# Attention stage of a fused kernel: probability tiles turned three slots behind their scores and ahead of the products, the scalar engine copying head 2 of four

## The chip, the cores and the metric

The kernel runs on one core of a Trainium2 chip. The metric is the device time of one launch in microseconds. Five engines work side by side and meet only at semaphores: TensorE (PE; its weight loads are listed as PEld), VectorE (DVE), ScalarE (ACT), GpSimd (POOL) and the DMA queues, most of which SyncE (SP) issues here.

## The reference

One launch computes a cross-attention, a mixture of 64 experts, a second attention over the context and a dense feed-forward layer, on 8 batches of 256 tokens of width 512. The change lies in the first attention alone, 16 heads of width 32:

```python
q = rms_norm(linear(x, q_w, q_b), norm_q_w).reshape(B, L, NH, HD)
k_img = rms_norm(linear(ctx_img, k_img_w, k_img_b), norm_k_img_w).reshape(B, -1, NH, HD)
v_img = linear(ctx_img, v_img_w, v_img_b).reshape(B, -1, NH, HD)
scores = jnp.einsum('bqhd,bkhd->bhqk', q, k) * scale
probs = jax.nn.softmax(scores, axis=-1)
return jnp.einsum('bhqk,bkhd->bqhd', probs, v)
```

The context has 256 rows, all of them inside the first 257, so only the image branch has keys; the text branch is empty and adds nothing.

## The kernel before

The program is a row of stages (project, attend, route, place, experts, finish), each a block that all engines leave before the next begins. The change is inside `attend`, which in the profile lasts from 220.6 to 422.1 us.

`attend` works on 32 units (8 batches times 4 groups of four heads). A unit is done in two slots of two heads each, so there are 64 slots. For one slot `s` these steps follow each other:

- PE `scores` (line 319): four fp32 matmuls with 32 rows of contraction, two query halves of two heads, into `pS[s % 2]`; they wait until ACT has read slot `s - 2`.
- DVE `tensor_reduce` (361): the minimum of the negated scores, step "M".
- ACT (395): four exponentials with their sums into `prob[s % 4]`, step "E".
- DVE `reciprocal` (366), step "R", written one slot later in DVE's program.
- POOL (415): two multiplications of `prob` by the reciprocal, one for each head, steps "N0" and "N1".
- PE `turn` (330): two halves (head 0 and head 1 of the slot) of four 128x128 transposes each, into `pT[0]` and `pT[1]`. Each half waits for POOL's step and until the half before it in the same `pT` has been copied out.
- the copies from `pT` to `probT`: DVE (375) or ACT (388).
- PE `products` (340), once for each unit, when all four heads lie in `probT`: eight fp32 matmuls with 32 output columns each into `pO`.
- ACT (404): `pO` to `qT`, whose columns are free by then.

Each engine's program is written out by hand as a loop over slots; nothing reorders it. What stands behind a waiting instruction on its engine waits too. Before the change PE does, in slot `s`: `scores(s)`, then in odd slots `products` of unit `(s - 1) / 2 - 2`, then `turn(s - 2)`. DVE does M of `s`, R of `s - 1`, then the copies of slot `s - 2`; of the four heads of a unit it copies heads 0, 1 and 2. ACT copies head 3, which lies in `pT[1]`, at the head of the even slots (three slots behind), then does its exponentials.

In slots 8 to 11 ACT also does a copy of one quarter of the output weights (line 400), and in slots 12 to 15 POOL does the subtraction that goes with it (419). SP meanwhile writes 64 blocks of zeros and moves the weights of the last layer to another place in memory; these transfers wait for nothing in the loop over slots.

`Steps` counts a semaphore for one engine's named steps; `wait(eng, unit, name)` waits until the step of that unit has been done.

Of the kernel before, what the change touches and what calls it, by code (L numbers as in the profile page):

```python
# [28 lines left out]
ACT = mybir.ActivationFunctionType  # L29
# [4 lines left out]
T = B * S  # L34
# [4 lines left out]
HG = P // HD  # L39
# [209 lines left out]
def attend(nc, a, qT, kT, V, Wraw, Wo, ident, y_dram, ffn_gu, ffn_d):  # L249
# [3 lines left out]

    GH, PAIR, UNITS = range(HG), 2, B * DC
    PAIRS = HG // PAIR
    SLOTS, BUFS = UNITS * PAIRS, 4
    slots = range(SLOTS + 5)
    with ExitStack() as ctx:
        sb = lambda name, shape, dt=F32: ctx.enter_context(nc.sbuf_tensor(name, shape, dt))
# [3 lines left out]
        probT = sb("probT", [P, 2, HG, TPB, S])  # L263
        pS = [ps(f"pS{i}", [P, PAIR, TPB, S]) for i in range(2)]
        pT = [ps(f"pT{j}", [P, TPB, S]) for j in range(PAIR)]
        pO = [ps(f"pO{j}", [P, S]) for j in range(2)]
        peS, peO = Steps(nc, ctx, "a_peS", ["S"]), Steps(nc, ctx, "a_peO", ["O"])
        peT = Steps(nc, ctx, "a_peT", ["T0", "T1"])
        dveM, dveR = Steps(nc, ctx, "a_dveM", ["M"]), Steps(nc, ctx, "a_dveR", ["R"])
        dveT, actT = Steps(nc, ctx, "a_dveT", ["T0", "T1", "T2"]), Steps(nc, ctx, "a_actT", ["T3"])  # L270
        actE, actO = Steps(nc, ctx, "a_actE", ["E"]), Steps(nc, ctx, "a_actO", ["O"])
        poolN = Steps(nc, ctx, "a_poolN", ["N0", "N1"])
        zero, s_zero, s_rest = sb("zero", [P, D]), ctx.enter_context(nc.semaphore("a_zero")), ctx.enter_context(nc.semaphore("a_rest"))
# [6 lines left out]
        @block.sync  # L280
        def _(eng):


            eng.dma_start(Wraw[:, :, :], a["attn_wT"][3]).then_inc(s_wo, 16)
            rest = y_dram.rearrange("(n p) d -> n p d", p=P)[T * K // P:NBLK]
            eng.wait_ge(s_zero, 1)
            for n in range(NBLK - T * K // P):
                eng.dma_start(rest[n], zero[:, :]).then_inc(s_rest, 16)

            half = DC * F  # L290
            eng.dma_start(ffn_gu[:, 0:half], a["ffn_gT"].rearrange("p c f -> p (c f)")).then_inc(s_words, 16)
            eng.dma_start(ffn_gu[:, half:2 * half], a["ffn_uT"].rearrange("p c f -> p (c f)")).then_inc(s_words, 16)
            eng.dma_start(ffn_d, a["ffn_dT"].rearrange("p f d -> p (f d)")).then_inc(s_words, 16)
            eng.wait_ge(s_rest, 16 * (NBLK - T * K // P))
            eng.wait_ge(s_words, 48)

        def place_of(s):
            u, x = divmod(s, PAIRS)
            return u, x, u // DC, u % DC

        def turned(eng, u, j):

            if j < HG - 1:
                dveT.wait(eng, u, f"T{j}")
            else:
                actT.wait(eng, u, "T3")

        @block.tensor
        def _(eng):
            for x in (peS, peT, peO):  # L310
                x.start(eng)

            def scores(s):
                u, x, b, g = place_of(s)
                actE.wait(eng, s - 2, "E")
                for h in range(TPB):
                    for i in range(PAIR):
                        rows = bass.ts(x * PAIR + i, HD)
                        m = eng.matmul(pS[s % 2][:, i, h, :], qT[rows, g, b * S + h * P:b * S + (h + 1) * P], kT[rows, g, bass.ts(b, S)],
                                       start=True, stop=True)  # L320
                peS.done(m, "S")

            def turn(s):
                u, x, b, g = place_of(s)
                for i in range(PAIR):
                    poolN.wait(eng, s, f"N{i}")
                    turned(eng, (s - 1) // PAIRS, (s - 1) % PAIRS * PAIR + i)
                    for kt in range(TPB):
                        for h in range(TPB):
                            m = eng.transpose(pT[i][:, kt, bass.ts(h, P)], prob[:, s % BUFS, i, h, bass.ts(kt, P)], ident[:, :])  # L330
                    peT.done(m, f"T{i}")

            def products(u):
                b, g = u // DC, u % DC
                actO.wait(eng, u - 2, "O")
                for j in GH:
                    turned(eng, u, j)
                for kt in range(TPB):
                    for j in GH:
                        m = eng.matmul(pO[u % 2][bass.ts(j, HD), :], V[:, b * TPB + kt, g * P + j * HD:g * P + (j + 1) * HD],  # L340
                                       probT[:, u % 2, j, kt, :], start=kt == 0, stop=kt == TPB - 1)
                peO.done(m, "O")

            for s in slots:
                if s < SLOTS:
                    scores(s)
                if s % PAIRS == 1 and 0 <= s // PAIRS - 2 < UNITS:
                    products(s // PAIRS - 2)
                if 0 <= s - 2 < SLOTS:
                    turn(s - 2)  # L350

        @block.vector
        def _(eng):
            for x in (dveM, dveR, dveT):
                x.start(eng)

            for s in slots:
                if s < SLOTS:
                    peS.wait(eng, s, "S")
                    actE.wait(eng, s - BUFS, "E")  # L360
                    dveM.done(eng.tensor_reduce(low[:, s % BUFS, :, :], pS[s % 2][:, :, :, :], axis=AX.X, op=ALU.min), "M")  # L361
                r = s - 1
                if 0 <= r < SLOTS:
                    actE.wait(eng, r, "E")
                    poolN.wait(eng, r - BUFS, "N1")
                    dveR.done(eng.reciprocal(inv[:, r % BUFS, :, :], tot[:, r % BUFS, :, :]), "R")  # L366
                c = s - 2
                if 0 <= c < SLOTS:
                    u, x, b, g = place_of(c)
                    for i in range(PAIR):  # L370
                        j = x * PAIR + i
                        if j < HG - 1:
                            peT.wait(eng, c, f"T{i}")
                            peO.wait(eng, u - 2, "O")
                            dveT.done(eng.tensor_copy(probT[:, u % 2, j, :, :], pT[i][:, :, :]), f"T{j}")

        @block.scalar
        def _(eng):
            for x in (actE, actT, actO):
                x.start(eng)  # L380

            for s in slots:
                c = s - 3
                if 0 <= c < SLOTS and c % PAIRS == PAIRS - 1:
                    u, x, b, g = place_of(c)
                    peT.wait(eng, c, f"T{PAIR - 1}")
                    peO.wait(eng, u - 2, "O")
                    actT.done(eng.activation(probT[:, u % 2, HG - 1, :, :], pT[PAIR - 1][:, :, :], ACT.Copy), "T3")
                if s < SLOTS:
                    dveM.wait(eng, s, "M")  # L390
                    peT.wait(eng, s - BUFS, f"T{PAIR - 1}")
                    dveR.wait(eng, s - BUFS, "R")
                    for i in range(PAIR):
                        for h in range(TPB):
                            e = eng.activation(prob[:, s % BUFS, i, h, :], pS[s % 2][:, i, h, :], ACT.Exp, bias=low[:, s % BUFS, i, h:h + 1],  # L395
                                               scale=-1.0, accum_out=tot[:, s % BUFS, i, h:h + 1])
                    actE.done(e, "E")
                if s in HIGHS:
                    eng.wait_ge(s_wo, 16)
                    eng.activation(Wo[0][:, s - HIGHS[0], :], Wraw[:, s - HIGHS[0], :], ACT.Copy).then_inc(s_high, 1)  # L400
                if s % PAIRS == 0 and 0 <= s // PAIRS - 3 < UNITS:
                    u = s // PAIRS - 3
                    peO.wait(eng, u, "O")
                    actO.done(eng.activation(qT[:, u % DC, bass.ts(u // DC, S)], pO[u % 2][:, :], ACT.Copy), "O")
# [1353 lines left out]
```

## Time and profile before

| | us |
|---|---|
| median of three runs | 1659.73 |
| the runs | 1667.11, 1659.73, 1653.78 |
| the profiled execution | 1676.87 |
| its span | 1675.0 |
| `attend` within it | 201.5 |
| PE busy over the span | 1470.4 |
| DVE, ACT, POOL busy over the span | 1026.8, 869.5, 630.1 |

How to read it: the durations in the rows below are those of the profiled execution, which is 17.1 us longer than the median of the runs. The three runs lie 13.3 us apart. A busy PE is not PE at its peak, since the ends of pipelined matmuls are modelled; the distance from one start to the next is what the engine's program took. "Idle before" names the releaser that came last by the profile. The chain that ended last, part 4 of the page, covers 30% of the span and lies in the last stage, so it says nothing of `attend`. TensorE's granted clock is 1.00 at full speed, which is 2.4 GHz, and 0.50 at 1.2 GHz.

### The profile page before, as it was taken

The page shows a single profiled execution, that of the slowest core. Times are in us where ns is not written, and L with a number is a line of the kernel's source. Part 1 is how long each engine was busy: PE and PEld are TensorE (multiplying, and loading weights), DVE is VectorE, ACT ScalarE, POOL GpSimd, SP SyncE. Part 2 cuts the span into 40 slices and gives each one's busy share as a digit, 9 for nine tenths or more (in the row PEclk, how much of TensorE's full clock was granted, in tenths as well). Part 3 has the DMA queues.
Part 4 walks back from the last instruction along what each step waited for, and adds up shares of the span by engine and source line. Part 5 has one row for each costly group of instructions (what it writes and reads, how often), then busy time and mean ns, then how long its engine had stood idle before and what let it go on. Part 6 is the DMA issues. An engine that isn't in the chain of part 4 may idle for free. (4 is left out here: it accounts for less than half of the span.)

```text
span 1675.0 us, 37963 instructions
## 1 busy us (share of the span) xinstructions
PE 1470.4 (88%) x8537; PEld 1170.0 (70%) x8538; DVE 1026.8 (61%) x2055; ACT 869.5 (52%) x1988; POOL 630.1 (38%) x717
## 2 busy tenths in 40 slices
PE   2999989999884399999999999999981579999999
PEld 1545555665672298888888888888871468888888
DVE  3343446787568757667677666666634456667732
ACT  0222247888337556666666666666640234444442
POOL 2212136777114232232223323222316476666322
PEclk9999968999995599999999999999995789999999
DMA  5000079000117158877877777777637444444200
GB/s 225 25 19 25 19 275 359 2 1 2 48 57 295 44 166 280 276 270 261 277 268 266 270 263 248 263 252 263 221 109 251 130 148 134 138 135 135 81 13 26
DMA packets 90247, 273.83 MB, mean 163 GB/s; under 512 B 12421, under 2 KB 12550, under 8 KB 88966
## 3 DMA queue, kind: packets, MB, share of 16 engines
q1 hardware_dynamic: 66070, 191.80, 32.5%
q0 software_dynamic: 23680, 77.61, 15.4%
q10 hardware_dynamic: 432, 3.67, 0.5%
q8 instruction: 26, 0.43, 0.1%
q14 instruction: 39, 0.32, 0.1%
HBM read 204.88 MB, written 76.81 MB: 168 GB/s over the span
## 5 line engine op out<-in xcount | busy, mean ns | idle before, releaser
L974 POOL DMA_INDIRECT xg<-h_rows,idx x168 | 184.8, 1100 | 463.6 <-PE m_x L1002 454.4
L1017 PE MATMUL m_g<-wgu_high,bxTh 128*128 x660 | 236.2, 358 | 2.2 <-DVE bxTl L1090 2.1
L1017 PE MATMUL m_g<-wgu_low,bxTh 128*128 x660 | 223.5, 339 | 0.0
L1017 PE MATMUL m_g<-wgu_high,bxTl 128*128 x660 | 223.3, 338 | 0.0
L1420 PE MATMUL f_g<-x4T_high,ffn_gu 128*128 128x256 f32 x704 | 176.5, 292 | 14.5 <-issue 12.2
L1420 PE MATMUL f_g<-x4T_low,ffn_gu 128*128 128x256 f32 x704 | 169.3, 282 | 0.0
L1090 DVE TENSOR_TENSOR bxTl<-m_x,bxTh 128x512 fp32r<-128x512 f32 x166 | 114.8, 692 | 84.6 <-ACT bxTh L1159 64.2
L852 DVE TENSOR_TENSOR wgu_low<-raw_gu,wgu_high x61 | 107.3, 1759 | 82.9 <-ACT wgu_high L842 81.7
L1311 POOL DMA_INDIRECT G<-y_rows,slot x128 | 135.3, 1057 | 56.6 <-issue 50.5
L415 POOL TENSOR_TENSOR prob<-prob,inv 128x512 f32<-128x512 f32 x128 | 130.5, 1041 | 62.8 <-DVE inv L366 62.8
L1177 ACT ACTIVATE y<-m_y 128x512 f32<-128x512 f32 x164 | 98.3, 600 | 105.9 <-PE m_y L1037 91.1
L1037 PE MATMUL m_y<-wd_high,hidTm 128*128 x328 | 144.4, 440 | 7.6 <-issue 5.2
L1420 PEld LDWEIGHTS f_g<-x4T_high,ffn_gu 128*128 128x128 f32 x704 | 134.5, 191 | 20.4 <-issue 16.8
L395 ACT ACTIVATE prob<-pS,low 128x256 f32<-128x256 f32 x256 | 118.1, 475 | 44.8 <-DVE low L361 44.8
L1420 PEld LDWEIGHTS f_g<-x4T_low,ffn_gu 128*128 128x128 f32 x704 | 134.7, 191 | 2.0 <-issue 1.7
L1037 PE MATMUL m_y<-wd_low,hidTm 128*128 x328 | 129.9, 396 | 0.0
L1017 PEld LDWEIGHTS m_g<-wgu_high,bxTh 128*128 128x128 f32 x660 | 124.4, 188 | 3.4 <-issue 2.8
L1017 PEld LDWEIGHTS m_g<-wgu_low,bxTh 128*128 128x128 f32 x660 | 124.9, 189 | 0.0
L1017 PEld LDWEIGHTS m_g<-wgu_high,bxTl 128*128 128x128 f32 x660 | 124.5, 189 | 0.0
L1159 ACT ACTIVATE bxTh<-m_x 128x512 fp32r<-128x512 f32 x166 | 99.1, 597 | 47.6 <-issue 45.2
L1474 DVE SCALAR_TENSOR_TENSOR X<-G,w,X 128x512 f32 (+1 forms) x128 | 106.1, 869 | 15.3 <-DMA G<-y_rows,slot 14.6
L1317 POOL TENSOR_TENSOR hT_low<-f_hid,hT_high 128x256 fp32r<-128x256 f32 x88 | 66.7, 759 | 116.8 <-ACT hT_high L1658 115.7
(240 smaller groups left out, 3222.4 us busy)
## 6 DMA issues: line engine op xcount, KB each, us to landing
raw_gu<-in_exp_gu SPq DMA_DIRECT2D x64, 768.0 KB, 6.8
y_rows<-y SPq DMA_DIRECT2D x164, 256.0 KB
raw_d<-in_exp_d SPq DMA_DIRECT2D x64, 512.0 KB, 7.7
y_rows<-zero SPq DMA_DIRECT2D x64, 256.0 KB, 3.5
ffn_gu<-ffn_gu_words SPq DMA_DIRECT2D x1, 5632.0 KB
X<-in_x SPq DMA_DIRECT2D x4, 1024.0 KB, 17.8
ctxT<-in_ctxT SPq DMA_DIRECT2D x16, 256.0 KB, 2.6
h_rows<-h SPq DMA_DIRECT2D x16, 256.0 KB, 2.0
```

What stands on the lines that cost most here:

```text
L395: e = eng.activation(prob[:, s % BUFS, i, h, :], pS[s % 2][:, i, h, :], ACT.Exp, bias=low[:, s % BUFS, i, h:h + 1], scale=-1.0, accum_out= ...
L415: poolN.done(eng.tensor_tensor(w, w, inv[:, s % BUFS, i, :].unsqueeze(2).to_broadcast([P, TPB, S]), ALU.mult), f"N{i}")
L852: eng.tensor_tensor(self.gu[1][:, at, :], self.raw_gu[:, at, :], self.gu[0][:, at, :].bitcast(F32), ALU.subtract).then_inc(self.s_low_gu, 1)
L974: eng.indirect_dma_start(xg[:, u, :].bitcast(F32), None, h_dram, bass.IndirectOffsetOnAxis(ap=idx[half][:, u:u + 1], axis=0)).then_inc(s_g ...
L1017: m = eng.matmul(pg[u % 2][:, 0:2 * I], xT[l][:, u % 2, c, :], W.gu[r][:, buf * DC + c, :], start=c == 0 and n == 0, stop=c == DC - 1 and ...
L1037: m = eng.matmul(py[par][:, :], left, right, start=n == 0, stop=n == 4)
L1090: dveX.done(eng.tensor_tensor(xT[1][:, u % 2, :, :], px[u % 2][:, :].rearrange("p (c n) -> p c n", c=DC), xT[0][:, u % 2, :, :].bitcast(F3 ...
L1159: actX.done(eng.activation(xT[0][:, u % 2, :, :], px[u % 2][:, :].rearrange("p (c n) -> p c n", c=DC), ACT.Copy), "xTh")
L1177: actY.done(eng.activation(y[:, u % 2, :], py[u % 2][:, :], ACT.Copy), "y")
L1311: eng.indirect_dma_start(G[:, i, k, :], None, y_dram, bass.IndirectOffsetOnAxis(ap=slot8[:, t, k:k + 1], axis=0)).then_inc(s_g[i][k], 16)
L1420: m = eng.matmul(pgu[f % 2][:, bass.ts(n, S)], Wgu[:, n, c, bass.ts(f, P)].bitcast(way), x[:, c, :].bitcast(way), start=c == 0 and part == ...
L1474: dveA.done(eng.scalar_tensor_tensor(X[:, t, :], G[:, i, k, :], w8[:, t, k:k + 1], X[:, t, :], ALU.mult, ALU.add), f"k{k}_{i}")
```

## The change

PE turns slot `s - 3` in slot `s`, and does so right after the scores; the products come last in the odd slots. DVE's copies go along and are three slots behind too. ACT copies head 2 of each unit (in `pT[0]`) and DVE heads 0, 1 and 3. ACT's copy was three slots behind the scores already: it stood one slot behind its turn and now stands in the same slot as its turn.

```diff
--- before.py
+++ after.py
@@ -253,7 +253,9 @@
 
     GH, PAIR, UNITS = range(HG), 2, B * DC
     PAIRS = HG // PAIR
-    SLOTS, BUFS = UNITS * PAIRS, 4
+    SLOTS, BUFS, TURN = UNITS * PAIRS, 4, 3
+
+    ACT_HEAD = 2
     slots = range(SLOTS + 5)
     with ExitStack() as ctx:
         sb = lambda name, shape, dt=F32: ctx.enter_context(nc.sbuf_tensor(name, shape, dt))
@@ -267,7 +269,7 @@
         peS, peO = Steps(nc, ctx, "a_peS", ["S"]), Steps(nc, ctx, "a_peO", ["O"])
         peT = Steps(nc, ctx, "a_peT", ["T0", "T1"])
         dveM, dveR = Steps(nc, ctx, "a_dveM", ["M"]), Steps(nc, ctx, "a_dveR", ["R"])
-        dveT, actT = Steps(nc, ctx, "a_dveT", ["T0", "T1", "T2"]), Steps(nc, ctx, "a_actT", ["T3"])
+        dveT, actT = Steps(nc, ctx, "a_dveT", [f"T{j}" for j in GH if j != ACT_HEAD]), Steps(nc, ctx, "a_actT", [f"T{ACT_HEAD}"])
         actE, actO = Steps(nc, ctx, "a_actE", ["E"]), Steps(nc, ctx, "a_actO", ["O"])
         poolN = Steps(nc, ctx, "a_poolN", ["N0", "N1"])
         zero, s_zero, s_rest = sb("zero", [P, D]), ctx.enter_context(nc.semaphore("a_zero")), ctx.enter_context(nc.semaphore("a_rest"))
@@ -300,10 +302,7 @@
 
         def turned(eng, u, j):
 
-            if j < HG - 1:
-                dveT.wait(eng, u, f"T{j}")
-            else:
-                actT.wait(eng, u, "T3")
+            (actT if j == ACT_HEAD else dveT).wait(eng, u, f"T{j}")
 
         @block.tensor
         def _(eng):
@@ -344,10 +343,10 @@
             for s in slots:
                 if s < SLOTS:
                     scores(s)
+                if 0 <= s - TURN < SLOTS:
+                    turn(s - TURN)
                 if s % PAIRS == 1 and 0 <= s // PAIRS - 2 < UNITS:
                     products(s // PAIRS - 2)
-                if 0 <= s - 2 < SLOTS:
-                    turn(s - 2)
 
         @block.vector
         def _(eng):
@@ -364,12 +363,12 @@
                     actE.wait(eng, r, "E")
                     poolN.wait(eng, r - BUFS, "N1")
                     dveR.done(eng.reciprocal(inv[:, r % BUFS, :, :], tot[:, r % BUFS, :, :]), "R")
-                c = s - 2
+                c = s - TURN
                 if 0 <= c < SLOTS:
                     u, x, b, g = place_of(c)
                     for i in range(PAIR):
                         j = x * PAIR + i
-                        if j < HG - 1:
+                        if j != ACT_HEAD:
                             peT.wait(eng, c, f"T{i}")
                             peO.wait(eng, u - 2, "O")
                             dveT.done(eng.tensor_copy(probT[:, u % 2, j, :, :], pT[i][:, :, :]), f"T{j}")
@@ -380,12 +379,12 @@
                 x.start(eng)
 
             for s in slots:
-                c = s - 3
-                if 0 <= c < SLOTS and c % PAIRS == PAIRS - 1:
+                c = s - TURN
+                if 0 <= c < SLOTS and c % PAIRS == ACT_HEAD // PAIR:
                     u, x, b, g = place_of(c)
-                    peT.wait(eng, c, f"T{PAIR - 1}")
+                    peT.wait(eng, c, f"T{ACT_HEAD % PAIR}")
                     peO.wait(eng, u - 2, "O")
-                    actT.done(eng.activation(probT[:, u % 2, HG - 1, :, :], pT[PAIR - 1][:, :, :], ACT.Copy), "T3")
+                    actT.done(eng.activation(probT[:, u % 2, ACT_HEAD, :, :], pT[ACT_HEAD % PAIR][:, :, :], ACT.Copy), f"T{ACT_HEAD}")
                 if s < SLOTS:
                     dveM.wait(eng, s, "M")
                     peT.wait(eng, s - BUFS, f"T{PAIR - 1}")
```

The order on PE, in the middle of the stage. `pS` are the scores, `pT` the turned probabilities, `pO` the products; `a_actT` and `a_dveT` are the copies out of `pT` by ACT and DVE, `a_poolN` the multiplications, `a_actE` the exponentials. Before, from the products of an odd slot to the turn of the even slot behind it:

```order
L340 MATMUL pO0<-probT,V 32x256 [waits a_dveT,a_actT,a_actO]
L340 MATMUL pO0<-probT,V 32x256 x7
L330 MATMUL pT0<-ident,prob 128x128 [waits a_dveT,a_poolN]
L330 MATMUL pT0<-ident,prob 128x128 x3
L330 MATMUL pT1<-ident,prob 128x128 [waits a_dveT,a_poolN]
L330 MATMUL pT1<-ident,prob 128x128 x3
L319 MATMUL pS0<-kT,qT 128x256 [waits a_actE]
L319 MATMUL pS0<-kT,qT 128x256 x3
L330 MATMUL pT0<-ident,prob 128x128 [waits a_dveT,a_poolN]
L330 MATMUL pT0<-ident,prob 128x128 x3
L330 MATMUL pT1<-ident,prob 128x128 [waits a_actT,a_poolN]
L330 MATMUL pT1<-ident,prob 128x128 x3
```

And with the change, from the turn of an odd slot to the turn of the even slot behind it:

```order
L329 MATMUL pT0<-ident,prob 128x128 [waits a_actT,a_poolN]
L329 MATMUL pT0<-ident,prob 128x128 x3
L329 MATMUL pT1<-ident,prob 128x128 [waits a_dveT,a_poolN]
L329 MATMUL pT1<-ident,prob 128x128 x3
L339 MATMUL pO0<-probT,V 32x256 [waits a_actT,a_dveT,a_actO]
L339 MATMUL pO0<-probT,V 32x256 x7
L318 MATMUL pS0<-kT,qT 128x256 [waits a_actE]
L318 MATMUL pS0<-kT,qT 128x256 x3
L329 MATMUL pT0<-ident,prob 128x128 [waits a_dveT,a_poolN]
L329 MATMUL pT0<-ident,prob 128x128 x3
L329 MATMUL pT1<-ident,prob 128x128 [waits a_dveT,a_poolN]
L329 MATMUL pT1<-ident,prob 128x128 x3
```

The products have moved from ahead of the odd slot's turn to behind it. The wait on ACT's copy has moved from the second half (`pT1`) of the even slot's turn to the first half (`pT0`) of the odd slot's turn.

The order on ACT, from an odd slot's exponentials over one even slot. Before:

```order
L395 ACTIVATE prob,tot<-pS1,low 128x256 [waits a_dveR,a_peT,a_dveM]
L395 ACTIVATE prob,tot<-pS1,low 128x256 x3
L388 ACTIVATE probT<-pT1 128x512 [waits a_peO,a_peT]
L395 ACTIVATE prob,tot<-pS0,low 128x256 [waits a_dveR,a_peT,a_dveM]
L395 ACTIVATE prob,tot<-pS0,low 128x256 x3
L404 ACTIVATE qT<-pO1 128x256 [waits a_peO]
```

And with the change:

```order
L394 ACTIVATE prob,tot<-pS1,low 128x256 [waits a_dveR,a_peT,a_dveM]
L394 ACTIVATE prob,tot<-pS1,low 128x256 x3
L387 ACTIVATE probT<-pT0 128x512 [waits a_peO,a_peT]
L394 ACTIVATE prob,tot<-pS0,low 128x256 [waits a_dveR,a_peT,a_dveM]
L394 ACTIVATE prob,tot<-pS0,low 128x256 x3
L403 ACTIVATE qT<-pO1 128x256 [waits a_peO]
```

The rows stand in the same order; the copy reads `pT0` in place of `pT1`, and its wait on the turning is for the slot that PE works on at the same time.

## Rows read from the trace of the kernel before

**Rows 1.** Windows: stretch, length, busy PE, PEld, DVE, ACT, POOL; PEclk, DMA share, GB/s.

```profile
220.60:422.10 201.50, 188.53 (x1536) 121.62 (x1536) 143.89 (x224) 151.70 (x581) 135.44 (x133) 0.90 0.38 133
224.00:261.00 37.00, 35.95 (x174) 23.23 (x175) 17.84 (x29) 20.60 (x82) 17.68 (x18) 0.50 1.04 393
261.00:291.76 30.76, 27.89 (x237) 17.63 (x236) 22.02 (x34) 23.11 (x87) 23.80 (x23) 0.94 1.03 347
291.76:414.21 122.45, 118.04 (x1060) 76.51 (x1056) 98.55 (x155) 101.80 (x396) 89.66 (x88) 1.00 0.02 6
```

**Rows 2.** Waits, 292 to 414 us: us in total, times, longest us.

```profile
PEld pT L330 <- POOL prob L415: 9.0, 22, 0.4
...
PE pT L330 <- ACT probT L388: 4.4, 22, 0.2
```

**Rows 3.** Timeline, PE, one unit: start us, us, engine, line, operation [idle before].

```profile
337.31 1.13 PE L319 MATMUL pS<-kT,qT 32*128 32x256 f32 x8
338.37 0.66 PE L330 MATMUL pT<-ident,prob 128*128 128x128 f32 x4
339.23 0.63 PE L330 MATMUL pT<-ident,prob 128*128 128x128 f32 x4 [0.20 <-ACT probT L388]
339.79 1.13 PE L319 MATMUL pS<-kT,qT 32*128 32x256 f32 x8
340.85 1.07 PE L340 MATMUL pO<-probT,V 128*32 128x256 f32 x16
341.85 1.09 PE L330 MATMUL pT<-ident,prob 128*128 128x128 f32 x8
342.88 0.48 PE L319 MATMUL pS<-kT,qT 32*128 32x256 f32 x2
```

**Rows 4.** Timeline of the weight loads (PEld), same stretch.

```profile
341.85 0.86 PEld L330 LDWEIGHTS pT<-ident,prob 128*128 128x128 f32 x8 [0.41 <-issue]
342.88 0.30 PEld L319 LDWEIGHTS pS<-kT,qT 32*128 32x128 f32 x4 [0.17 <-issue]
```

**Rows 5.** Timeline, DVE, same stretch.

```profile
338.49 1.23 DVE L361 TENSOR_REDUCE low<-pS 128x4 f32<-128x1024 f32 x1 [0.82 <-PE pS L319]
339.63 0.17 DVE L366 RECIPROCAL inv<-tot 128x4 f32<-128x4 f32 x1
339.71 1.26 DVE L375 COPY probT<-pT 128x512 f32<-128x512 f32 x2
...
342.55 0.69 DVE L375 COPY probT<-pT 128x512 f32<-128x512 f32 x1 [0.27 <-PE pT L330]
```

**Rows 6.** Timeline, ACT, same stretch.

```profile
338.48 0.61 ACT L388 ACTIVATE probT<-pT 128x512 f32<-128x512 f32 x1
339.75 0.47 ACT L395 ACTIVATE prob<-pS,low 128x256 f32<-128x256 f32 x1 [0.66 <-DVE low L361]
```

**Rows 7.** Timeline, POOL, 336 to 343 us.

```profile
336.79 2.04 POOL L415 TENSOR_TENSOR prob<-prob,inv 128x512 f32<-128x512 f32 x2 [0.44 <-DVE inv L366]
339.88 2.04 POOL L415 TENSOR_TENSOR prob<-prob,inv 128x512 f32<-128x512 f32 x2 [1.05 <-DVE inv L366]
```

**Rows 8.** Line 419: count, ns min/median/max, first and last start.

```profile
L419 POOL TENSOR_TENSOR wo_low<-wo_raw,wo_high x4: 1262/1266/1271, 274.7 to 285.8; 128x512 fp32r<-128x512 f32 x4
```

**Rows 9.** Timeline, PE, head of the stage.

```profile
225.04 2.08 PE L319 MATMUL pS<-kT,qT 32*128 32x256 f32 x8 [3.25 <-ACT prob L395]
...
236.77 2.08 PE L319 MATMUL pS<-kT,qT 32*128 32x256 f32 x8
...
246.45 2.08 PE L319 MATMUL pS<-kT,qT 32*128 32x256 f32 x8
```

**Rows 10.** Timeline, PE, between the head and the even stretch.

```profile
265.56 1.18 PE L330 MATMUL pT<-ident,prob 128*128 128x128 f32 x8
...
269.55 0.63 PE L330 MATMUL pT<-ident,prob 128*128 128x128 f32 x4 [1.17 <-ACT probT L388]
...
271.21 1.93 PE L340 MATMUL pO<-probT,V 128*32 128x256 f32 x16
```

## The prediction

> **What bounds the kernel now.** The page first: part 4, the chain that ended last, lies in the last stage, so what `attend` is worth has to be read from the stage itself. The table of windows gives it: `attend` lasts 201.5 us of the span's 1675.0, and has three parts [rows 1]. Up to 261 us PE runs at half clock (0.50) and is busy 35.95 of 37 us. From 261 to 291.76 the pace is uneven. From 291.76 to 414.21 every unit is like the one before, at clock 1.00.
>
> Next the waits of the even part. PE's turn waits once in each unit, 22 times: 0.2 us put down to ACT's copy, 0.4 us in the row of the weight loads put down to POOL [rows 2]. The timeline of PE shows the place [rows 3]. A unit takes 342.88 - 337.31 = 5.57 us from scores to scores. Start to start its blocks take: scores 1.06 (337.31 to 338.37), even turn 1.42 (338.37 to 339.79), scores 1.06, products 1.00, odd turn 1.03 (341.85 to 342.88). Both turns are the same eight transposes, so 0.39 us of the even one is wait. The second half waits for two things that arrive nearly together: ACT's copy of head 3 begins at 338.48 and ends at 339.09 [rows 6], and POOL's second step ends at 336.79 + 2.04 = 338.83 [rows 7], 0.40 before the start at 339.23. Everything else on PE follows without a wait. So PE bounds this part, and what can be had is 5.57 - 0.39 = 5.18 us a unit.
>
> **The change, in the even part.** Nothing is added or removed: the counts of matmuls, copies and exponentials stay. Let an even slot's scores start at 0 under the new order. By the unwaited blocks of [rows 3] PE starts the even turn at 1.06, its second half at 1.57 (half of 1.03), the odd scores at 2.09, the odd turn at 3.15 and 3.66, the products at 4.18 and the next unit at 5.18. Is each input there?
>
> - POOL's steps: PE turns slot s - 3. R of a slot runs in the next slot's DVE program, 1.14 us after M's start (339.63 - 338.49) [rows 5], M 1.18 after the scores (338.49 - 337.31) [rows 3, 5]. POOL starts 0.25 later and takes 2.04 for both heads [rows 7]. R of the odd slot thus starts at 5.18 + 2.32 = 7.50, N1 ends at 9.79, and PE, which here started 0.40 after POOL's end, wants it at 10.36 + 1.57 = 11.93. The cushion is 1.7 us where there was none.
> - DVE: in the even slot M from 1.18, R at 2.32, the one copy (head 3) from 2.40 to 3.09 (copy 0.69, 0.08 behind R) [rows 5]. A copy's end needs 0.14 us to reach PE (339.09 to 339.23) [rows 3, 6]: 3.23, wanted at 3.66. Cushion 0.43, the smallest. In the odd slot its two copies end at 5.18 and 5.75, wanted at 6.24 and 6.75.
> - ACT: the first half's output can be read 0.70 after its start (341.85 to 342.55) [rows 3, 5], at 1.76. Head 2 is copied by 2.37 (0.61 [rows 6]), reaches PE at 2.51 and is wanted at 3.15. The exponentials behind it could not start before M at 1.18 + 1.26 (338.49 to 339.75 [rows 5, 6]) = 2.44, so the copy fits in front of them. Were head 3 still ACT's, head 2 would be DVE's and arrive at 3.23 for 3.15, 0.08 us late.
> - The reverse waits: exponentials of slot s reuse the buffer turned in slot s - 1, done before the scores of s. The products of unit u - 2 are over two slots before `probT` is rewritten. Both cost nothing; the next to be late would be DVE's copy of head 3.
>
> The one transition that the trace lacks is products followed by scores. The products before a turn took 1.00 with a gap of 0.41 in the weight loads, while a turn before scores has a gap of 0.17 [rows 4]. So products before scores cost between 1.00 - 0.24 = 0.76 and 1.00; as a bound above I take 1.06, what scores took. I use 1.00, the row of the same instructions: a unit is 4.94 to 5.24, taken as **5.18**. The Trainium skill (TensorE: Matmul & The Clock Gate, Part 3, The mechanism) says that a weight load passes matmuls in flight only where its row group differs. The products use all rows and so would hold the next weights back before scores as before a turn: 5.18 by the rule, 4.94 by the other end.
>
> **The sum**, against the profiled execution of 1676.87 us:
>
> - Even part: 122.45 us for 22 units at 5.57 [rows 1], less 22 x 5.18 = 113.96: **8.5**.
> - Uneven part: from the turn at 265.56 [rows 10] to 291.76 are four units in 26.2 us, less 20.7 = 5.5. It holds a wait of 1.17 us on ACT and, behind it, a stretch at half speed in which the products took 1.93 instead of 1.07 [rows 3, 10]; both go with the wait. It also holds POOL's four subtractions of 1.27 us [rows 8]. They stay: 2.04 + 1.27 = 3.31 in slots of 2.59 puts POOL 4 x 0.72 = 2.9 us behind, the cushion takes 1.7 to 1.8, and 1.1 remains. **4.4**.
> - Half-clock part: PE waits nowhere between 225.04 and 261 [rows 9], so nothing there; but one turn fewer stands ahead of the last scores: **1.0**.
> - End: ACT's copy now holds the first half of the turn behind the last exponentials, where it held the second half: half of the turn's 1.03, **-0.5**.
> - Other stages start earlier by the sum and change in nothing else. SP's transfers leave DMA at 0.02 after 292 [rows 1], 120 us before the end of `attend`: 0.
>
> 8.5 + 4.4 + 1.0 - 0.5 = **13.4 us**, 0.8%. The profiled execution would become 1663.5. It lies 17.1 above the median of the three runs; the same gain from 1659.73 gives **1646**.
>
> One more reading bears on the size. PE's busy time in the even part is 118.04 of 122.45 us [rows 1], which shows only 4.4 us of idle; start to start it is 8.5, because the modelled ends overlap the next start. The Trainium skill (Trainium Kernel Development and Optimization, Performance Expectations) calls matmul busy time a bad metric for the distance to the limit. By busy time the first term would be 4.4 and the sum 9.3; by starts it is 13.4.
>
> **Rivals.**
>
> - *A cheaper unit* (chance 0.13). With products before scores at 0.76, 26 full-speed units gain 0.24 each more: 6.2, in all 19.6, 1640. For it: scores use 32 rows of the array. Against: the 0.41 gap stands wherever products are followed by anything. ACT and DVE, busy 4.63 and 4.48 a unit [rows 1], would allow it.
> - *A new wait takes back part* (0.14). The smallest cushion is 0.43 us, on DVE, whose chain scores, M, R, copy has to fit between two turns. If releases come 0.6 later than I put them, 0.2 a unit is lost: 26 x 0.2 = 5.2, gain 8, 1652. Against: every latency in it is read from a row.
> - *The change does not remove what costs* (0.06). If the longer even turn is mostly the pipeline and not the wait, the gain is the turn at the head and little else: 2 us, 1658. Against: the same eight transposes take 1.03 one slot later.
> - *Slower* (0.07): the half-clock part at the head lasts longer. The clock fell as PE waited 3.25 us for the first exponentials before 225.04 [rows 9] and came back at 261 [rows 1]. That wait stays, and the blocks behind it come in another order. A unit at half clock takes 246.45 - 236.77 = 9.68 [rows 9], 4.5 more than 5.18. From three more units in that state (29 us on top of the 36 there are) the change is slower than before; seven more would make 1659.73 - 13.4 + 7 x 4.5 = 1678. Against: in the changed order PE still never waits there.
>
> The forecast has 0.60. About 1% (16.6 us) is what a measurement of this kernel can tell from no change; the three runs span 13.3 us, so the medians alone move the result by some 5. Range: 1633 (the cheaper unit with 7 us of scatter) to 1658 (the change that removes little); the likeliest case's own is 1639 to 1654. Faster by over 1% means below 1643.1: the cheaper unit nearly always (0.11) and about a third of the forecast's share by scatter (0.21), together 0.32. Slower by over 1%: 0.04. Within 1%: 0.64.
>
> **What would show it.** In the profile of the changed kernel: scores to scores 5.18 a unit in the even part; no row of PE's turn waiting for ACT or POOL there; waits on POOL only beside the four subtractions; PE starts of products then scores 1.00 apart; no half-speed stretch behind slot 12; `attend` 188 us. It would be wrong if DVE's or ACT's copies appear as what ended PE's waits, if the unit is still over 5.4, or if the clock at the head returns later than some 40 us after the stage begins.

## The result, and the profile after

| | before | with the change |
|---|---|---|
| median | 1660.06 us (7 runs) | 1646.49 us (7 runs) |
| range of the runs | 1653.78 to 1667.11 | 1642.54 to 1646.91 |
| ratio, 95% interval | | 0.991, 0.9884 to 0.9936 |
| profiled execution, its span | 1676.87, 1675.0 | 1644.26, 1642.3 |
| `attend` in it | 201.5 | 177.9 |

One of the seven executions of the changed kernel, 1744.53 us at a granted clock of 0.817 over the whole run, is left out of the range and the ratio but not of the median (1645.93 without it); the others had 0.943 to 0.946. The gain is 15 us by the ratio (10.6 to 19.3 by its interval) and 13.6 by the medians. In the profiled executions `attend` alone is 23.6 us shorter, 201.5 to 177.9 where 188 was forecast. That is more than the times gain; why is the subject of the last experiments.

The windows of the changed kernel, with the same parts as [rows 1] has; columns: stretch, length, busy us of PE, PEld, DVE, ACT and POOL, then PEclk, DMA share, GB/s:

```profile
220.17:398.10 177.93, 172.02 (x1536) 115.71 (x1536) 141.33 (x224) 150.72 (x581) 135.20 (x133) 0.95 0.42 151
224.00:239.40 15.40, 14.82 (x72) 10.03 (x72) 8.65 (x14) 10.33 (x44) 9.82 (x10) 0.51 1.03 389
239.40:279.00 39.60, 38.87 (x362) 26.05 (x354) 31.90 (x50) 34.45 (x133) 33.29 (x33) 1.00 1.03 374
279.00:389.71 110.71, 110.71 (x1025) 74.99 (x1024) 94.07 (x151) 99.09 (x387) 87.46 (x87) 1.00 0.14 46
```

The part at half clock lasts 17.1 us in place of 37.5 (222.1 to 239.2, where it was 223.3 to 260.9), and from 279 us on PE is busy in all of its 110.71 us: the waits of [rows 2] are gone. One unit on PE, to be laid beside [rows 3] (start us, us, engine, line, operation):

```profile
338.98 1.13 PE L318 MATMUL pS<-kT,qT 32*128 32x256 f32 x8
340.04 1.09 PE L329 MATMUL pT<-ident,prob 128*128 128x128 f32 x8
341.06 1.13 PE L318 MATMUL pS<-kT,qT 32*128 32x256 f32 x8
342.13 1.09 PE L329 MATMUL pT<-ident,prob 128*128 128x128 f32 x8
343.15 1.07 PE L339 MATMUL pO<-probT,V 128*32 128x256 f32 x16
344.15 0.70 PE L318 MATMUL pS<-kT,qT 32*128 32x256 f32 x4
```

From scores to scores it is 344.15 - 338.98 = 5.17 us. Scores 1.06, turn 1.02, scores 1.07, turn 1.02, products 1.00: every block at the length that it had unwaited before. The weight loads of the same unit answer [rows 4]:

```profile
338.98 0.73 PEld L318 LDWEIGHTS pS<-kT,qT 32*128 32x128 f32 x8 [0.41 <-issue]
...
341.06 0.73 PEld L318 LDWEIGHTS pS<-kT,qT 32*128 32x128 f32 x8 [0.17 <-issue]
...
343.15 0.59 PEld L339 LDWEIGHTS pO<-probT,V 128*32 128x32 f32 x16 [0.17 <-issue]
```

Behind the products, ahead of the even slot's scores (338.98), the gap is 0.41 us, as it was ahead of a turn. The transition that the trace before lacked, products followed by scores, costs what was taken for it. DVE and ACT, beside [rows 5, 6]:

```profile
340.16 1.23 DVE L360 TENSOR_REDUCE low<-pS 128x4 f32<-128x1024 f32 x1 [0.58 <-PE pS L318]
341.30 0.17 DVE L365 RECIPROCAL inv<-tot 128x4 f32<-128x4 f32 x1
341.38 0.66 DVE L374 COPY probT<-pT 128x512 f32<-128x512 f32 x1
342.24 1.22 DVE L360 TENSOR_REDUCE low<-pS 128x4 f32<-128x1024 f32 x1 [0.20 <-PE pS L318]
```

```profile
340.74 0.60 ACT L387 ACTIVATE probT<-pT 128x512 f32<-128x512 f32 x1 [0.47 <-PE pT L329]
341.42 0.47 ACT L394 ACTIVATE prob<-pS,low 128x256 f32<-128x256 f32 x1
```

ACT's copy begins 1.76 us after the even scores and its exponentials 2.44 after them, both as worked out. DVE's single copy ends at 342.04, 3.06 after the scores; the half turn that needs its buffer starts at about 342.64. PE waits in the middle of the stage in only one place, where POOL does its four subtractions:

```profile
272.79 1.13 PE L318 MATMUL pS<-kT,qT 32*128 32x256 f32 x8
274.32 0.66 PE L329 MATMUL pT<-ident,prob 128*128 128x128 f32 x4 [0.39 <-POOL prob L414]
275.31 0.66 PE L329 MATMUL pT<-ident,prob 128*128 128x128 f32 x4 [0.34 <-POOL prob L414]
275.90 1.07 PE L339 MATMUL pO<-probT,V 128*32 128x256 f32 x16
```

The scores are followed by the turn after 1.53 us in place of 1.06, and the two halves lie 0.99 and 0.59 apart in place of 0.51 each: 1.0 us in all, beside a unit of 5.17 one of 6.19. And the head of the stage, beside [rows 9]:

```profile
224.58 3.90 PE L318 MATMUL pS<-kT,qT 32*128 32x256 f32 x16 [3.25 <-ACT prob L394]
...
236.22 1.97 PE L329 MATMUL pT<-ident,prob 128*128 128x128 f32 x8
238.12 1.57 PE L339 MATMUL pO<-probT,V 128*32 128x256 f32 x16
239.62 1.13 PE L318 MATMUL pS<-kT,qT 32*128 32x256 f32 x8
```

Full speed comes back during the products at 238.12. The kernel before had it back at 261.

### The profile page after: what moved, and what is told of

The parts are those of the page before. It is cut to its first block and busy times, and to the rows that moved or that the text cites. A ratio compares the mean times of both kernels' runs of the same rounds, so it can differ in the third digit from the quotient of the medians.

```text
span 1642.3 us, 37963 instructions
## 1 busy us (share of the span) xinstructions
PE 1454.9 (89%) x8537; PEld 1166.4 (71%) x8538; DVE 1023.1 (62%) x2055; ACT 866.3 (53%) x1988; POOL 627.6 (38%) x717
## 5 line engine op out<-in xcount | busy, mean ns | idle before, releaser
L973 POOL DMA_INDIRECT xg<-h_rows,idx x168 | 188.3, 1121 | 460.1 <-PE m_x L1001 451.1
L1473 DVE SCALAR_TENSOR_TENSOR X<-G,w,X 128x512 f32 (+1 forms) x128 | 105.7, 865 | 13.9 <-DMA G<-y_rows,slot 13.6
```

Source lines behind the costliest of these rows:

```text
L973: eng.indirect_dma_start(xg[:, u, :].bitcast(F32), None, h_dram, bass.IndirectOffsetOnAxis(ap=idx[half][:, u:u + 1], axis=0)).then_inc(s_g ...
L1473: dveA.done(eng.scalar_tensor_tensor(X[:, t, :], G[:, i, k, :], w8[:, t, k:k + 1], X[:, t, :], ALU.mult, ALU.add), f"k{k}_{i}")
```

## The experiments

**Three more readings of the kernel before**: one comes first here, two at the end.

> The kernel before, once more, for a second reading of the stretch at half clock. Theory A (the change takes a wait of 0.39 us out of each unit; how long PE stays at half clock at the head is chance): the even part again has 5.57 us a unit, and the stretch at half clock at the head is some length between 12 and 40 us, not bound to 36. Rival B (the new order on PE brings the clock back sooner): 5.57 us a unit, and the stretch at half clock is again 33 to 40 us, beside 16 with the change.

1661.54 us. The even part has 5.56 us a unit, as before. Half clock at the head lasted 27.3 us (224.2 to 251.5) and came back for 3.4 us at 261.8, so 37 is no fixed length; it is also not 17. That lies within theory A's 12 to 40 us and outside rival B's 33 to 40.

**The three parts of the change, each alone.** First the order on PE:

```diff
+                if 0 <= s - 2 < SLOTS:
+                    turn(s - 2)
                 if s % PAIRS == 1 and 0 <= s // PAIRS - 2 < UNITS:
                     products(s // PAIRS - 2)
-                if 0 <= s - 2 < SLOTS:
-                    turn(s - 2)
```

> The kernel before with the turn ahead of the products in odd slots, still two slots behind, ACT copying head 3. Theory A: PE's wait comes from POOL's two steps being late, and this order asks for them 1.0 us sooner, so the turn of the odd slot waits too (0.8 and 0.5 us by adding up the latencies) and the unit grows from 5.57 to about 6.4 us; over 26 units 20 to 25 us slower, 1680 to 1685. Rival C (the longer even turn is the pipeline of PE, and what counts is which block follows which): the unit is 5.4 to 5.6 and the time 1655 to 1662.

1673.9 us, ratio 1.0077 (1.0044 to 1.0109); a unit takes 6.25 us. PE in one odd slot and the even scores behind it:

```profile
332.68 1.13 PE L319 MATMUL pS<-kT,qT 32*128 32x256 f32 x8
334.26 0.66 PE L330 MATMUL pT<-ident,prob 128*128 128x128 f32 x4 [0.45 <-DVE probT L375]
335.25 0.66 PE L330 MATMUL pT<-ident,prob 128*128 128x128 f32 x4 [0.34 <-POOL prob L415]
335.84 1.07 PE L340 MATMUL pO<-probT,V 128*32 128x256 f32 x16
336.84 1.13 PE L319 MATMUL pS<-kT,qT 32*128 32x256 f32 x8
```

The turn starts 1.58 after the scores in place of 1.06 and its halves lie 0.99 and 0.59 apart. Both wait for POOL, although the row names DVE for the first: POOL's two steps start at 333.16 and end at 334.20 and 335.20, 0.06 and 0.05 us before the halves, and the DVE copy that is named had ended at about 333.7. Moving the turn ahead of the products without giving POOL its slot costs 0.7 us a unit: slower, as theory A had it, though by 9.5 us of the medians (1664.44 before) and not by 20 to 25. Part of what is missing lies in the clock: this kernel had 20.5 us at half clock in its trace, and beside the reading of before with the same 20.5 us its `attend` is 16.9 us longer (209.6 against 192.7). Rival C falls: the blocks are the same and in the order of the changed kernel.

Next the head that ACT copies (`ACT_HEAD = 2`), with the distance of two slots and the old order:

```diff
-                        if j < HG - 1:
+                        if j != ACT_HEAD:
...
-                    actT.done(eng.activation(probT[:, u % 2, HG - 1, :, :], pT[PAIR - 1][:, :, :], ACT.Copy), "T3")
+                    actT.done(eng.activation(probT[:, u % 2, ACT_HEAD, :, :], pT[ACT_HEAD % PAIR][:, :, :], ACT.Copy), f"T{ACT_HEAD}")
```

> The kernel before with ACT copying head 2 in place of head 3, nothing else. Theory A: ACT's copy stands behind the exponentials as before (its end reaches PE 1.92 us after the even slot's scores by the latencies), but the first half of the even turn wants it at 1.06, so PE waits 0.86 in place of 0.39 and the unit is 6.04 us; 1670 to 1675. Rival: the copy of either head costs the same, 5.57 a unit and no change.

1674.7 us, ratio 1.0071 (1.0045 to 1.0098), 6.00 us a unit:

```profile
335.39 1.13 PE L318 MATMUL pS<-kT,qT 32*128 32x256 f32 x8
337.31 1.06 PE L329 MATMUL pT<-ident,prob 128*128 128x128 f32 x8 [0.79 <-ACT probT L387]
338.31 1.13 PE L318 MATMUL pS<-kT,qT 32*128 32x256 f32 x8
```

PE's even turn starts 1.92 us after the scores, the latency added up from the rows of before to the hundredth, and waits for ACT's copy. So two of the three edits are losses if made alone. The third, turning and copying three slots behind with the old order and ACT on head 3, as an edit of the changed kernel:

```diff
-    ACT_HEAD = 2
+    ACT_HEAD = 3
...
-                if 0 <= s - TURN < SLOTS:
-                    turn(s - TURN)
                 if s % PAIRS == 1 and 0 <= s // PAIRS - 2 < UNITS:
                     products(s // PAIRS - 2)
+                if 0 <= s - TURN < SLOTS:
+                    turn(s - TURN)
```

> Turn and copies three slots behind the scores, but products still ahead of the turn and head 3 still ACT's. Theory A: POOL's steps get a slot of cushion, so nearly all of the gain is here: 5.27 us a unit, since head 2, now DVE's and copied in the slot just ahead of the products, reaches PE at 3.23 us where 3.15 is wanted, a wait of about 0.1 us at the products; time 1648 to 1651. Rival D (the order matters as much as the distance): the unit stays at 5.4 or more and the time at 1654 or more.

1648.47 us, ratio 0.9918 (0.9888 to 0.9949), 5.35 us a unit. Of 5.56 - 5.17 = 0.39 us, 0.21 come from the distance alone. What is left is at the products:

```profile
333.76 1.13 PE L318 MATMUL pS<-kT,qT 32*128 32x256 f32 x8
335.00 1.07 PE L339 MATMUL pO<-probT,V 128*32 128x256 f32 x16
```

1.24 us from scores to products in place of 1.06: 0.18 of wait, where 0.09 was expected. The profile names no releaser for it. By the times it is head 2, which DVE copied after the minimum and the reciprocal of the slot just before: the copy runs from 334.08 to 334.74, and the products start 0.26 us behind its end, where 0.14 had been reckoned, the time from a copy to the turn that reuses its buffer. Rival D falls narrowly (5.4 us or more): the distance alone gives half of the gain. With the new order as well, and still head 3 on ACT:

```diff
-    ACT_HEAD = 2
+    ACT_HEAD = 3
```

> The changed kernel with head 3 on ACT in place of head 2. Theory A: 5.27 us a unit against 5.18: the first half of the odd turn waits 0.1 us for DVE's copy of head 2, as the latencies added up to 3.23 for 3.15. Time about 2 us above the changed kernel, 1648 to 1650. Rival E (ACT's copy of head 3 comes later than that of head 2 and holds the exponentials back, so that the unit is bound by ACT): 5.4 us or more a unit, 1653 or more.

1644.18 us, ratio 0.9882 (0.9851 to 0.9913), 5.21 us a unit:

```profile
333.03 1.13 PE L318 MATMUL pS<-kT,qT 32*128 32x256 f32 x8
334.15 1.06 PE L329 MATMUL pT<-ident,prob 128*128 128x128 f32 x8
```

1.12 from scores to turn, so 0.06 of wait, and 0.04 on the unit. DVE's copy of head 2 ends at 334.01, 0.14 before the turn. Rival E falls. This step is too small for the times: these runs have a lower median than the changed kernel's (1646.49, and 1648 to 1650 was expected here), although its unit is longer.

**The clock at the head.** Four fp32 matmuls fill PE's gap of 3.25 us ahead of the third slot's scores. They take 3.63 us, so those scores come 0.3 us later than without them; they write `pT[0]`, which nothing has used yet, and nobody reads what they write:

```diff
+            def keep_warm(n):
+                for _ in range(n):
+                    eng.matmul(pT[0][:, :, :], ident[:, :], V[:, 0, :], start=True, stop=True)
             for s in slots:
+                if s == 2:
+                    keep_warm(4)
                 if s < SLOTS:
                     scores(s)
```

> The kernel before plus four fp32 matmuls (512 columns each, 3.4 us at full clock) on PE ahead of the third slot's scores, where PE waits 3.25 us for the first exponentials; their output is never read. Theory A (the clock falls because of that wait, whatever the order): no half clock at the head, the first units at 5.6 to 6.5 us in place of 9.68, 12 to 18 us off the time: 1643 to 1650, and the runs lie closer together than the 15 us of the kernel before. Rival F (the clock falls for what PE does in this stage, 32-row scores and transposes, not for the wait): half clock comes at the head all the same, and the time stays within 3 us of before or grows by the 3.4 us of the matmuls.

> The same four matmuls in the changed kernel. Theory A: its 17 us at half clock go as well; a unit there takes 9.68 in place of 5.18, so 17 us at half clock cost about 8 us: 1636 to 1640, and the difference between this and the kernel before with the four matmuls is what the change is worth at equal clock, 12 to 14 us. Rival B (the change works mostly by bringing the clock back sooner): with the clock held up in both, they are under 8 us apart. Rival F: no gain, 1646 to 1650.

With them the kernel before took 1661.12 us, ratio 0.9952 (0.9925 to 0.9979) to the kernel before beside it (1667.92), and the changed one 1644.18, ratio 0.9845 (0.9807 to 0.9883). The head of the kernel before with the four matmuls, on PE:

```profile
219.75 1.16 PE L319 MATMUL pS<-kT,qT 32*128 32x256 f32 x16 [1.53 <-ACTq L61]
220.84 3.70 PE L346 MATMUL pT<-V,ident 128*128 128x512 f32 x8
224.47 1.13 PE L319 MATMUL pS<-kT,qT 32*128 32x256 f32 x8
225.54 0.66 PE L330 MATMUL pT<-ident,prob 128*128 128x128 f32 x4
226.49 0.66 PE L330 MATMUL pT<-ident,prob 128*128 128x128 f32 x4 [0.30 <-POOL prob L421]
```

Scores take 1.07 and not 2.01 us, and the first three units, from the third slot on, 5.25, 6.01 and 5.55 us and not 9.68. The windows over all of `attend`, of the kernel before with the four matmuls and then of the changed one with them:

```profile
219.75:406.45 186.70, 175.07 (x1544) 112.17 (x1544) 143.72 (x224) 151.17 (x581) 135.21 (x133) 1.00 0.40 143
```

```profile
219.90:392.77 172.87, 169.04 (x1544) 112.72 (x1544) 141.31 (x224) 151.19 (x581) 135.34 (x133) 1.00 0.44 155
```

Both have a granted clock of 1.00, and `attend` takes 186.70 and 172.87 us: at equal clock the change is worth **13.8 us** in `attend`. The medians of the two kernels are 16.9 us apart; the 3 us beyond 13.8 are not explained; the runs of each lie 12 and 7 us apart. Rival B's figure for this pair, under 8 us, is not met: most of the gain is the waits. Rival F falls: without the wait the stage's own matmuls don't bring the clock down here. How long it stays down once it has fallen is another question, taken up below. The expected size was missed: the kernel before gained 6.8 us by the medians and not 12 to 18, since I had reckoned with 37 us at half clock as the rule, and its runs still spread over 12 us. The changed kernel gained 6.9 us against its own median beside it, 1651.03, where about 8 and a time of 1636 to 1640 were expected.

> The changed kernel once more, on this chip and beside these runs. Theory A: time 1643 to 1648; in the profile 5.18 us a unit, one loss of about 1 us where POOL's four subtractions are, and half clock at the head for some length that is chance. Rival B: half clock at the head again 17 us.

1651.03 us, above what was expected, but so was the kernel before beside it (1667.92): ratio 0.9895 (0.9847 to 0.9942). The profile repeats: 5.17 us a unit, one unit of 6.20, half clock for 17.1 us, `attend` 177.84.

> The kernel before, a third reading of its half-clock stretches. So far the head had 37.6 and 27.3 us with the kernel before and 17.1 us in all five kernels that turn three slots behind. Theory A (chance): 17 us or less can come up here as well as 37. Rival B (turning later shortens it): over 24 us again.

> The same, a fourth reading: theory A, any length; rival B, over 24 us.

1663.15 us with 27.3 us at half clock and another 3.4 behind it, and 1658.88 us with 20.5 us. The windows from 220 to 275 us, of the third reading, the fourth, and of the changed kernel's second one:

```profile
220.00:275.00 55.00, 49.41 (x328) 31.69 (x328) 32.79 (x50) 36.40 (x136) 30.01 (x30) 0.72 1.01 368
```

```profile
220.00:275.00 55.00, 49.02 (x368) 32.08 (x367) 36.86 (x57) 40.68 (x154) 35.02 (x34) 0.81 1.02 373
```

```profile
220.00:275.00 55.00, 51.00 (x404) 34.22 (x398) 41.29 (x64) 45.20 (x175) 39.97 (x39) 0.84 1.02 371
```

Clock 0.72 and 0.81 against 0.84. So the four readings of the kernel before have 37.5, 27.3, 27.3 and 20.5 us at the head and, three of them, 3.4 us more at 261 to 271; the two others that turn two slots behind have 20.5 each at the head (head 2 alone 6.8 more at 262). All five readings of kernels that turn three slots behind (the changed kernel twice, the two with head 3 on ACT, and the next experiment) have 17.1 and nothing more within `attend`. Rival B is right in that, and theory A's "chance" is not the whole of it; but B's own figures were missed too, 27.3 us for 33 to 40 and 20.5 for over 24. What in the program ends the stretch at the head sooner was not taken apart.

The second stretch can be followed further. In each of the four traces that have one, PE had waited 1.17 us (kernel before) or 1.30 us (head 2 alone) for ACT's copy, in the slots with ACT's extra work, and the clock fell within 1.6 us of the end of that wait. In the other ten no wait of PE between 240 us and the last scores is above 0.86 us, and in the kernels that turn three slots behind none is above 0.40. So this stretch goes with a wait that the change removes. Not every such wait brings it: head 2 alone has another of 1.30 us, before 255.57, without a fall.

**POOL's subtractions further apart:**

```diff
-        HIGHS, LOWS = range(8, 8 + DC), range(12, 12 + DC)
+        HIGHS, LOWS = range(8, 8 + DC), range(12, 12 + 4 * DC, 4)
...
-                    c = s - LOWS[0]
+                    c = LOWS.index(s)
```

> The changed kernel with POOL's four subtractions in slots 12, 16, 20 and 24 in place of 12 to 15. Theory A: 1.27 us in every fourth slot fits into POOL's idle time (1.04 us a unit), so PE's one remaining wait in the middle of the stage (about 1 us by the profile) goes and nothing else changes: attend 1.0 us shorter at equal clock, not visible in the time. Rival: the subtraction delays the multiplications wherever it stands, and PE waits four times.

The unit of 6.19 is gone, none behind the head is above 5.25, and `attend` takes 177.09 us, 0.8 less than 177.94 and 177.84. The time, 1653.06 with ratio 0.9882 (0.9836 to 0.9928), can't show it: the profiled execution of 1655.74 us has a last stage of 417.0 us where that of the changed kernel has 406.3.

**Both additions to the changed kernel:**

> The changed kernel with both additions, the four matmuls in PE's gap at the head and POOL's subtractions in slots 12, 16, 20 and 24: the version that should beat both. Theory A: attend 172.87 - 1.0 = 171.9 us, and about 6 us off the changed kernel, ratio to the kernel before 0.983 to 0.987. Rival: what is gained in attend is lost in the stages behind it, ratio 0.99.

```profile
220.05:391.85 171.80, 168.71 (x1544) 112.86 (x1544) 140.98 (x224) 150.83 (x581) 135.14 (x133) 1.00 0.44 156
```

`attend` takes 171.80 us. The time is 1638.7 us, ratio 0.9847 (0.9819 to 0.9875): the fastest of all, 23 us under the kernel before beside it (1661.91). Its six runs lie within 5 us, where the kernel before's seventeen spread over 19.

## Why the prediction was right, and where it was not

The time, 1646.49 for 1646, is closer than the reasoning deserves: a sum of 13.4 us against 13.6 by the medians and 15 by the ratio, while `attend` in the profile came to 177.9 us where 188 was forecast. Step by step:

- *One wait of 0.39 us in each unit, put down to two releasers; the unit becomes 5.18.* The size is right: 5.17, no wait left in the even part. The share of the two releasers is not. POOL's step was taken to need 0.40 us to reach PE; with the order alone the halves start 0.05 to 0.06 us after it. So in the kernel before, POOL's step, ended at 338.83 [rows 7], would have let the half start at about 338.89, just when it was wanted (338.37 + 0.51), and the whole wait was for ACT's copy, which ended 0.14 before the start. POOL had no cushion but cost nothing. The parts made alone show both: asking for the turn sooner makes POOL late (6.25 us a unit), wanting ACT's copy a half turn sooner makes PE wait longer for it (6.00), and turning a slot later serves both and gets half of the gain.
- *Products ahead of scores cost 1.00.* Right, gap 0.41. The rival of a cheaper unit falls. The Trainium skill (TensorE: Matmul & The Clock Gate, Part 3, The mechanism) says that a weight load passes matmuls in flight only where its row group differs; by that rule the unit was to be 5.18, and the trace's 5.17 agrees with it.
- *Cushions.* ACT's copy and the exponentials came at 1.76 and 2.44 to the hundredth. DVE's smallest cushion was put at 0.43; its copy ended 3.06 after the scores where 3.09 was worked out. With head 3 on ACT 0.08 us late was said, and 0.06 measured. With the products ahead of the turn it was 0.18 for 0.09, because a latency of another pair of steps had been used. So sums of latencies are good to about 0.1 us here where each latency is that of the same two steps; POOL's, read off a start that waited for something else, was 0.35 too long.
- *Uneven part, 1.1 us left by POOL's subtractions.* 1.0 was measured, and spreading them removed 0.8.
- *One turn fewer ahead of the last scores, 1.0.* The row at 224.58 shows the scores of two slots without a turn between them; what that is worth was not measured by itself.
- *End, -0.5.* From the last scores to the end of `attend` it was 9.95 us and is 10.49.
- *The change doesn't remove what costs.* Fallen with 13.8 us at equal clock.
- *Half clock at the head: nothing.* This step failed. I priced a longer stretch as the slower rival and gave a shorter one no term, since PE waits nowhere in it. It became shorter: 17.1 us in place of 20.5 to 37.5 at the head. A unit of 9.68 in place of 5.18 makes 0.46 us for each us at half clock, so the 13.6 us less that the readings have on average (41.0, 30.7, 30.7 and 20.5 with what comes back later, against 17.1) are worth 6.3. With 13.8 that is 20.1, and the four readings' `attend` of 197.1 on average against 177.9 gives 19.2.

That the sum still met the time has two reasons. It counted 1.5 us (products and turn of 3.56 us between 271.21 and 274.77 in place of 2.03) for the short stretch at half speed, which belongs to the clock; without it 11.9 remain, and the four units that the head ran at half clock bring another 4 x 0.39 = 1.6 at full clock, 13.5 beside the 13.8 measured. And the times of the kernel before go with the clock: over the three groups of runs that stand beside the experiments, those at a mean granted clock of 0.945 or 0.946 took 1658 us on average, those at 0.937 or 0.938 took 1670, and two at 0.935 and 0.936 took 1680. Against runs at 0.943 to 0.946, the clock of the changed kernel's own in the first comparison, which took 1662 on average, its 1646.49 is a gain of 15 us; against 1670 it is 24. The profiled execution of before, 1676.87 us with 41 us at half clock in `attend`, was like the latter. `attend` is not the only place of the scatter: 6.7 of the 32.6 us between the two profiled executions lie in the last stage (413.0 and 406.3 us), which the change doesn't touch. It lasts 405 to 409 us in eleven of the fourteen traces, and 413.0, 417.2 and 417.0 in the three others (the kernel before, the same with the four matmuls, the changed kernel with the subtractions apart). So the 1646 was met in part by luck: with the shorter half clock, for which the sum has no term, `attend` became some 19 to 20 us shorter on average, and the executions that were compared differed by 15.

## What to carry to other kernels

Where an engine waits once in each turn of a hand-written loop, add up from the timeline when each input would arrive and when it would be wanted in the new order, to the hundredth: it gave the unit here before anything ran, and it told which of three edits lose time without the others. Take a latency only from a start that waited for nothing else. Compare at equal clock before crediting a change with the rest: filling the one wait that starts the half clock made 186.70 and 172.87 comparable. Here such a filling also took 7 us off each kernel's time.

## What the runs showed of the hardware

- PE fell to 1.2 GHz during a wait of 3.25 us, in all eleven traces that have it, and stayed there for 17 to 38 us although it then waited nowhere (busy 35.95 of 37 us [rows 1]). Four matmuls in the wait avoided the fall in all three kernels that had them, one trace each.
- In four traces it fell again for 3.4 or 6.8 us within 1.6 us of the end of a wait of 1.17 or 1.30 us; where no wait was above 0.86 us it did not fall again.
- How long it stays depends on the program as well as on the execution: 17.1 us in five of five readings with the turn three slots behind, 20.5 to 37.5 in six of six with two. Why stays open.
- A half turn started 0.05 to 0.06 us after the end of POOL's step that it waited for, 0.14 after the end of a copy out of its buffer, and the products started 0.26 after the end of the copy into `probT` (order alone, head 3 on ACT, distance alone).
- By the modelled ends PE is busy in 118.04 of 122.45 us [rows 1], 4.4 us of idle time, where start to start 8.5 us could be had.
